# First attention: one common step of four 32-row products subtracts the maxima of the third and fourth score tile

## The chip, the cores and the metric

One core of one Trainium2 chip runs the whole program. The metric is device time in microseconds (us), the median of three runs; lower is better. All engines of the core (TensorE, VectorE, ScalarE, GpSimd, and SyncE, which issues the DMAs) run instruction streams written out in the program, tied together by semaphores.

## What is computed

Two transformer-like layers over x (4 x 512 x 128): attention over the tokens and a small context, a mixture of experts, a second attention, a second mixture. The change touches the first attention alone: 16 heads of 64, so 8 pairs of heads for each of 4 batches, 32 pairs in all.

```python
def _L0_xattn_ref(x, latents, ...):            # x: the context (4, 32, 128), latents: the tokens (4, 512, 128)
    q = lat @ Wq
    kv_input = jnp.concatenate([x, lat], axis=1)
    k, v = jnp.split(kv_input @ Wkv, 2, axis=-1)
    ...
    dots = jnp.einsum('bhid,bhjd->bhij', q, k) * scale
    attn = jax.nn.softmax(dots, axis=-1)
    out = jnp.einsum('bhij,bhjd->bhid', attn, v)
    return out @ Wout
x = x + _L0_xattn_ref(...)
x = x + _L0_ffn_ref(...)
x = x + _L1_xattn_ref(...)
x = x + _L1_ffn_ref(...)
```

## The kernel before

**Order of the work.** The loop over the pairs i = 0 to 31 is one list, order_a, from which every engine's program takes its own steps. The string ITERATION sets the order in a pair; a name stands for a step of pair i (scores s0 to s3), of the next pair (qk, top scores t0 to t4, mt for max_turn) or of the pair before (pv p0 to p3, rows in even pairs from 2 on):

```python
"E A B PC CA0 C CA1 O0 ADD CS V qk p0 p1 t0 s0 t1 p2 t2 D s1 t3 p3 t4 P0 P2 s2 s3 rows mt O1 OUT O2 O3"
```

The other names are steps that come only in some pairs: PC and CS (the context's part), V (values of the next batch), B (the router's logits), OUT (the output projection), P0 and P2 (spreading one over the sums), C and D (layer norms and turns).

**Banks.** PSUM has 8 banks of 512 columns. Each step in TAKES_BANKS gets the next of three pairs of banks in turn (0 and 1, 2 and 3, 4 and 5), one bank for each head of a pair. Before it writes, TensorE waits for whoever last reads those banks (claim and release). s2, s3, mt and the next taker follow each other in this turn, so the next taker gets the banks of s2.

**The steps of a pair.** qk (L1423 to L1425, function three) makes queries and keys as three fp32r products of split numbers each; ScalarE rounds them (QH, KH, and QF: L843, L844, L847), VectorE forms the remainders (KL, QL: L1244, L1247). top (L1598, and L1605 for the context) computes the scores once with rounded numbers, VectorE takes the maxima over them (TOPS, L1254, L1256). max_turn combines them into one number for a query and head (TOPT, L1265, VectorE) and turns them into rows with four transposes (L1612, TensorE); ScalarE evicts them as TOPROW (L852). TOPT holds the first head's maximum at one column and the second head's 64 columns on, so that in TOPROW row 0 of each half of 64 rows is that head's maximum.

scores (L1631) makes one key tile of 128 keys of exact scores, transposed: four steps of two products, one for each head, on rows 0 to 63 and rows 64 to 127 of the array. Steps 0 to 2 are KH with QH, KL with QH and KH with QL; step 3 subtracts the maximum, as the product of MINUS (-1 in row 0 of each half, else 0) with TOPROW:

```python
lhs = (KH[r, k, c], KL[r, k, c], KH[r, k, c], MINUS[r, :])[step]
rhs = (QH[r, k, :], QH[r, k, :], QL[r, k, :], TOPROW[r, i % GROUP, :])[step]
last = pe.matmul(PSUM[:, place + h, :], lhs, rhs, start=step == 0, stop=step == 3)
```

ScalarE takes the exponential of each finished tile (PT, L866) from its two banks. GpSimd adds the exponentials of a pair over the key tiles (PSUMS, L690). pv (L1663) multiplies them with the values; rows (L1693, L1699, L1707) sums them; out (L1729) projects. context_scores (L1649) and context_sums (L1680) do the same for the 32 context rows; context_scores uses MINUS too.

**Constants.** GpSimd makes MINUS_F with one selection for each half (L593), ScalarE rounds it to MINUS (L820), both in the first 20 us.

Of the kernel before, what the change touches and what calls it, by code (L numbers as in the profile page):

```python
# [6 lines left out]
F32R = mybir.dt.float32r  # L7
I32 = mybir.dt.int32
U32 = mybir.dt.uint32
ALU = mybir.AluOpType  # L10
ACT = mybir.ActivationFunctionType
AX = mybir.AxisListType

P = 128
# [27 lines left out]
def build(nc, x, ctx, lnm_g, lnm_b, lnl_g, lnl_b, Wq, Wkv, Wout, rw, rb, w1, w2, cq, ckv, cc, Wr, Wg, Wu, Wd, out):  # L42
# [3 lines left out]
    DH = 64  # L46
# [6 lines left out]
    TPB = S // P  # L53
    NT = B * TPB
    KT = S // P
# [12 lines left out]
    GROUP = 4  # L68
# [5 lines left out]
    with ExitStack() as stack:  # L74
        def sb(name, *shape, dt=F32):
            return stack.enter_context(nc.sbuf_tensor(name, [P, *shape], dt))
# [14 lines left out]
        IDENT = sb("IDENT", P)  # L91
# [11 lines left out]
        KCF = sb("KCF", PAIRS, P)  # L103

        TOPS = sb("TOPS", TPB, 2, 2)
        TOPT = sb("TOPT", P + 16 * TPB)
        MINUS = sb("MINUS", P, dt=F32R)


        with ExitStack() as queries:  # L110
            QF = queries.enter_context(nc.sbuf_tensor("QF", [P, GROUP, S], F32))
            TOPROW = queries.enter_context(nc.sbuf_tensor("TOPROW", [P, GROUP, S], F32R))
# [14 lines left out]
        MINUS_F = PT[:, 2, 1, 0:P]  # L127
# [70 lines left out]
        PSUM = stack.enter_context(nc.psum_tensor("PSUM", [P, 8, BANK], F32))  # L198
# [13 lines left out]
        def dram(name, rows, width):  # L212
# [19 lines left out]


        CONST = Steps(sem("consts"), ["ident0", "ident", "half", "ones", "empty", "numbers", "topt", "minus0", "rows0", "spread0",
                                      "minus1", "minus2", "rows1", "rows", "rows_c0", "rows_c1", "rows_c", "iota2", "iota1",
                                      "spread1", "spread", "tie", "lower", "incl0", "incl", "run", "next"])
        s_lin = sem("lin")
        s_jp = sem("jp")
# [26 lines left out]
        s_const_r = sem("rounded_consts")  # L265
# [5 lines left out]
        s_top, s_max, s_comb = sem("top_scores"), sem("half_max"), sem("row_max")  # L271
        s_topt, s_toprow = sem("max_turned"), sem("max_rows")
        s_sc, s_exp = sem("scores"), sem("exps")
# [60 lines left out]
        for b in range(B + 1):  # L334
            i = b * PAIRS
# [13 lines left out]
            for g in (2 * b - 1, 2 * b):  # L349
                if g >= 0:  # L350

                    k = GROUP * (g + 1) + 1
# [35 lines left out]
        last = 2 * B - 1  # L388
# [18 lines left out]
        order_a, place, out_at, sums_at = [], 0, {}, {}  # L407
# [164 lines left out]
        def pool_program(pool):  # L572
# [7 lines left out]
            for which in range(2):  # L580
                last = pool.iota(NUMBERS[which], [[P, LIST_ROWS[which] // P]], base=(which + 1) * N, channel_multiplier=1)
# [3 lines left out]
            def constants():  # L585
                pool.memset(TOPT[:, :], 0.0).then_inc(CONST.sem, 1)
                pool.memset(MINUS_F, 0.0).then_inc(CONST.sem, 1)
                pool.memset(ROWS_F[:, :, :], 1.0).then_inc(CONST.sem, 1)
                pool.memset(SPREAD_F, 0.0).then_inc(CONST.sem, 1)

                for k in range(2):
                    pool.wait_ge(*CONST.at(0, f"minus{k}"))
                    pool.affine_select(out=MINUS_F, in_=MINUS_F, compare_op=ALU.not_equal, fill=-1.0, base=-64 * k,  # L593
                                       pattern=[[0, P]], channel_multiplier=1).then_inc(CONST.sem, 1)

                pool.wait_ge(*CONST.at(0, "rows0"))
                pool.memset(ROWS_F[:, 0:GROUP, 0:GROUP], 0.0).then_inc(CONST.sem, 1)
                pool.wait_ge(*CONST.at(0, "rows1"))
                for p in range(GROUP):
                    last = pool.memset(ROWS_F[:, p, p:p + 1], 1.0)  # L600
                last.then_inc(CONST.sem, 1)

                pool.memset(ROWS_F[:, GROUP, 0:GROUP], 1.0).then_inc(CONST.sem, 1)
                pool.wait_ge(*CONST.at(0, "rows_c0"))
                pool.affine_select(out=ROWS_F[:, GROUP, 0:GROUP], in_=ROWS_F[:, GROUP, 0:GROUP], compare_op=ALU.is_ge, fill=0.0,
                                   base=0, pattern=[[-M, GROUP]], channel_multiplier=1).then_inc(CONST.sem, 1)
                pool.wait_ge(*CONST.at(0, "rows_c1"))
                pool.affine_select(out=ROWS_F[:, GROUP, 0:GROUP], in_=ROWS_F[:, GROUP, 0:GROUP], compare_op=ALU.is_ge, fill=0.0,
                                   base=M - 1, pattern=[[M, GROUP]], channel_multiplier=-1).then_inc(CONST.sem, 1)
                pool.iota(TOKEN_INTS, [[S, B], [1, TPB]], base=0, channel_multiplier=TPB).then_inc(CONST.sem, 1)  # L610
                pool.iota(INTS[1][:, :], [[P, E * NT]], base=0, channel_multiplier=0).then_inc(CONST.sem, 1)

                for k in range(2):
                    pool.wait_ge(*CONST.at(0, f"spread{k}"))
                    for p in range(GROUP):
                        for half in range(2):
                            part = SPREAD_F[:, p, 64 * half:64 * half + 64]
                            last = pool.affine_select(out=part, in_=part, compare_op=ALU.not_equal, fill=1.0,
                                                      base=-(64 * k + 32 * half + p), pattern=[[0, 64]], channel_multiplier=1)
                    last.then_inc(CONST.sem, 1)  # L620
                for i in range(E):
                    last = pool.memset(TIE[:, :, i:i + 1], float(E - i))
                last.then_inc(CONST.sem, 1)
                pool.wait_ge(*CONST.at(0, "ones"))
                pool.affine_select(out=LOWER[:, :], in_=ONES[:, :], compare_op=ALU.is_gt, fill=0.0, base=0, pattern=[[1, P]],
                                   channel_multiplier=-1).then_inc(CONST.sem, 1)
                pool.memset(INCL[:, :, :], 1.0).then_inc(CONST.sem, 1)
                pool.wait_ge(*CONST.at(0, "incl0"))
                pool.affine_select(out=INCL[:, :, :], in_=INCL[:, :, :], compare_op=ALU.is_ge, fill=0.0, base=0,
                                   pattern=[[1, E], [-1, E]], channel_multiplier=0).then_inc(CONST.sem, 1)  # L630
                for which in range(2):
                    for i in range(E):
                        last = pool.memset(RUN[:, which, 0, i:i + 1], float(i * N))
                last.then_inc(CONST.sem, 1)
                pool.memset(NEXT[:, E - 1:E], float(N)).then_inc(CONST.sem, 1)
# [33 lines left out]
            for name, a, place, banks in order_a:  # L669
# [8 lines left out]
                elif name == "scores" and a[1] in ((1, 2, 3) if a[0] < ALL - 1 else (1,)):  # L678

                    i, kt = a  # L680
# [11 lines left out]
                elif name == "masks":  # L692
# [13 lines left out]
                    for c in range(4):  # L706
                        pool.wait_ge(*CMASKS.at(0, f"minus{c}"))
                        pool.affine_select(out=MINUSC.rearrange("p (h k) -> p h k", h=4), in_=MINUSC.rearrange("p (h k) -> p h k", h=4),
                                           compare_op=ALU.not_equal, fill=-1.0, base=-32 * c, pattern=[[-1, 4], [0, M]],
# [32 lines left out]
        def scalar_program(act):  # L742
# [73 lines left out]
            round_context_keys(0)  # L816
            split_features(0)
            round_weights(2, ld_wv)
            act.wait_ge(*CONST.at(0, "minus2"))
            act.activation(MINUS[:, :], MINUS_F, ACT.Copy).then_inc(s_const_r, 1)  # L820
            for name, a, place, banks in order_a:
                if name == "values":
                    b, kt = a
# [29 lines left out]
                elif name == "scores":  # L853
                    i, kt = a
# [19 lines left out]
                elif name == "pv" and a[1] == KT - 1:  # L874
                    i = a[0]
# [36 lines left out]
            for name, a in order_c:  # L912
# [13 lines left out]
                elif name == "c_scores":  # L926
# [3 lines left out]
                    for k in range(2):  # L930
                        act.activation(PT[:, 2 + a % 2, 2 * k:2 * k + 2, :], PSUM[:, 2 * k:2 * k + 2, :], ACT.Exp,
                                       scale=DC ** -0.5).then_inc(CPA[a].sem, 1)
# [15 lines left out]
        def vector_program(dve):  # L948
# [284 lines left out]
            for name, a, place, banks in order_a:  # L1233
# [14 lines left out]
                elif name == "top":  # L1248
                    i, c = a
# [9 lines left out]
                elif name == "max_turn":  # L1259
# [2 lines left out]
                        dve.wait_ge(s_topt, a)  # L1262
                    else:
                        dve.wait_ge(*CONST.at(0, "topt"))
                    dve.tensor_reduce(TOPT[:, 0:P].rearrange("p (h n) -> p n h", h=2)[:, 0:16 * TPB:16, :],  # L1265
                                      TOPS[:, :, :, :].rearrange("p t a h -> p t h a"), AX.X, ALU.max).then_inc(s_comb, 1)
                elif name == "one_over":
                    g, c = a
                    cols = slice(c * P, (c + 1) * P)
# [133 lines left out]
        def tensor_program(pe):  # L1403
# [142 lines left out]
            for name, a, place, banks in order_a:  # L1546
# [5 lines left out]
                elif name == "values":  # L1552
                    b, kt = a
                    k = b % 2
# [5 lines left out]
                    for n in range(2):  # L1560
                        c = slice(n * BANK, (n + 1) * BANK)
                        last = three(PSUM[:, place + n, :], XTH[:, k, cols], XTL[:, k, cols], WH[:, 2, c], WL[:, 2, c])
# [25 lines left out]
                elif name == "top":  # L1588


                    i, c = a
# [17 lines left out]
                elif name == "max_turn":  # L1609
                    pe.wait_ge(s_comb, a + 1)  # L1610
                    for t in range(TPB):
                        last = pe.transpose(PSUM[:, place, t * P:(t + 1) * P], TOPT[:, 16 * t:16 * t + P], IDENT[:, :])  # L1612
                    last.then_inc(s_topt, 1)
                    release(mine, (s_toprow, a + 1))
                elif name == "scores":
# [3 lines left out]
                    if kt == 0:  # L1619
                        pe.wait_ge(s_qkl, 2 * i + 2)  # L1620
                        if i == 0:
                            pe.wait_ge(s_const_r, 1)
                    for step in range(4):
                        if (kt, step) == (0, 3):
                            pe.wait_ge(s_toprow, i + 1)
                        for h in range(2):
                            r = slice(DH * h, DH * h + DH)
                            c = slice(kt * P, (kt + 1) * P)
                            lhs = (KH[r, k, c], KL[r, k, c], KH[r, k, c], MINUS[r, :])[step]
                            rhs = (QH[r, k, :], QH[r, k, :], QL[r, k, :], TOPROW[r, i % GROUP, :])[step]  # L1630
                            last = pe.matmul(PSUM[:, place + h, :], lhs, rhs, start=step == 0, stop=step == 3)  # L1631
                    last.then_inc(s_sc, 1)
                    release(mine, (s_exp, SCORED[name, a]))
                elif name == "context_scores":

# [264 lines left out]
```

## Time and profile before

| | us |
|---|---|
| runs | 784.04, 781.49, 780.24 (median 781.49) |
| profiled execution, its span from first to last instruction | 788.3 |
| TensorE busy in it | 706.3 |
| VectorE, ScalarE, GpSimd busy | 475.7, 378.0, 377.4 |

The profiled execution is one more execution, beside the three runs, and its own time is known by its span alone. Durations in the rows are those of one instruction or of a group; a matmul's duration runs from its issue to its last result, so that the next one starts before it ends. The granted clock is a share of TensorE's full speed, 2.4 GHz.

### The profile page before, as it was taken

The page shows a single profiled execution, that of the slowest core. Times are in us where ns is not written, and L with a number is a line of the kernel's source. Part 1 is how long each engine was busy: PE and PEld are TensorE (multiplying, and loading weights), DVE is VectorE, ACT ScalarE, POOL GpSimd, SP SyncE. Part 2 cuts the span into 40 slices and gives each one's busy share as a digit, 9 for nine tenths or more (in the row PEclk, how much of TensorE's full clock was granted, in tenths as well). Part 3 has the DMA queues.
Part 4 walks back from the last instruction along what each step waited for, and adds up shares of the span by engine and source line. Part 5 has one row for each costly group of instructions (what it writes and reads, how often), then busy time and mean ns, then how long its engine had stood idle before and what let it go on. Part 6 is the DMA issues. An engine that isn't in the chain of part 4 may idle for free.

```text
span 788.3 us, 13872 instructions
## 1 busy us (share of the span) xinstructions
PE 706.3 (90%) x4810; PEld 430.8 (55%) x4810; DVE 475.7 (60%) x966; ACT 378.0 (48%) x580; POOL 377.4 (48%) x361
## 2 busy tenths in 40 slices
PE   4899999999999999999999999997995687568991
PEld 3654555545556555556545545566995343336661
DVE  4745484585585875667477478465443386845553
ACT  4475554564654554655445444344552643223440
POOL 7264453473464475444464553634333304674552
PEclk9999999999999999999999999998998697569996
DMA  9999999990000000000030004301212500122325
GB/s 253 197 201 197 204 190 10 4 4 1 1 1 2 1 14 1 1 1 1 1 121 2 1 1 108 114 24 32 72 32 80 155 1 28 35 75 69 88 66 177
DMA packets 109867, 50.62 MB, mean 64 GB/s; under 512 B 44804, under 2 KB 103048, under 8 KB 109800
## 3 DMA queue, kind: packets, MB, share of 16 engines
q1 hardware_dynamic: 106280, 42.46, 36.0%
q0 software_dynamic: 3520, 7.27, 2.7%
q8 instruction: 42, 0.69, 0.4%
q14 instruction: 25, 0.20, 0.1%
HBM read 20.07 MB, written 29.64 MB: 63 GB/s over the span
## 4 chain that ended last, share of the span: by engine, by line
PE 74%; DVE 11%; issue 5%; ACT 3%; POOL 3%; DMA 2%; another core or an unknown queue 1%; SPq 1%; DVEq 0%; POOLq 0%; ACTq 0%
PE PSUM L1631 14%; PE PSUM L1663 13%; PE PSUM L1598 5%; PE PSUM L1463 5%; PE PSUM L1498 4%; PE PSUM L1468 4%; PE PSUM L1729 4%; PE PSUM L1423 3%; PE PSUM L1425 2%; PE PSUM L1424 2%; PE PSUM L1612 2%; PE PSUM L1605 2%; PE PSUM L1649 2%; PE PSUM L1693 2%; DVE REC L1377 1%
## 5 line engine op out<-in xcount | busy, mean ns | idle before, releaser
L866 ACT ACTIVATE PT<-PSUM 128x1024 f32<-128x1024 f32 x128 | 128.6, 1024 | 134.1 <-PE PSUM L1631 133.7
L690 POOL TENSOR_TENSOR PSUMS<-PT 128x1024 f32<-128x1024 f32 x32 | 76.0, 2376 | 210.4 <-ACT PT L866 171.4
L690 POOL TENSOR_TENSOR PSUMS<-PSUMS,PT 128x1024 f32<-128x1024 f32 x62 | 149.6, 2413 | 16.8 <-ACT PT L866 9.9
L1254 DVE TENSOR_REDUCE TOPS<-PSUM 128x2 f32<-128x1024 f32 x128 | 152.1, 1220 | 6.9 <-PE PSUM L1598 6.5
L1663 PE MATMUL PSUM<-PT,BIG 128*64 128x512 f32 x512 | 130.6, 611 | 0.0
L1209 DVE TENSOR_TENSOR SIL<-SIL,PSUM 128x256 f32<-128x256 f32 (+1 forms) x62 | 32.2, 519 | 65.7 <-ACT SIL L783 46.8
L1244 DVE TENSOR_TENSOR KL<-PSUM,KH 128x512 fp32r<-128x512 f32 x32 | 22.1, 691 | 68.2 <-ACT KH L844 67.7
L1598 PE MATMUL PSUM<-KH,QH 64*128 64x512 f32 x256 | 57.9, 449 | 4.0 <-DVE QL L1247 3.7
L1663 PEld LDWEIGHTS PSUM<-PT,BIG 128*64 128x64 f32 x512 | 28.4, 135 | 53.4 <-issue 52.0
L1598 PEld LDWEIGHTS PSUM<-KH,QH 64*128 64x128 f32 x256 | 24.2, 183 | 59.2 <-DVE TOPS L1254 24.9
L783 ACT ACTIVATE SIL<-PSUM 128x256 f32<-128x256 f32 (+1 forms) x62 | 28.6, 462 | 56.7 <-PE PSUM L1463 31.4
L1631 PE MATMUL PSUM<-QH,KH 64*128 64x512 f32 x256 | 54.8, 423 | 1.0 <-DVE QL L1247 0.7
L662 POOL DMA_INDIRECT results_d<-YS,XG x39 | 37.4, 958 | 29.4 <-DVE YS L1216 27.3
L1631 PE MATMUL PSUM<-TOPROW,MINUS 64*128 64x512 f32 x256 | 51.1, 393 | 0.0
L1631 PE MATMUL PSUM<-QH,KL 64*128 64x512 f32 x256 | 50.9, 391 | 0.0
L1631 PE MATMUL PSUM<-QL,KH 64*128 64x512 f32 x256 | 50.8, 390 | 0.0
L1463 PE MATMUL PSUM<-XGT,WS 128*128 128x128 f32 x368 | 46.8, 282 | 0.4 <-issue 0.4
L1463 PEld LDWEIGHTS PSUM<-XGT,WS 128*128 128x128 f32 x368 | 44.5, 198 | 1.0 <-issue 0.8
L1468 PE MATMUL PSUM<-BIG,XGT 128*128 x78 | 42.7, 631 | 1.9 <-DVE XGT L1201 1.9
L662 POOL DMA_INDIRECT results_b<-YS,XG x23 | 22.0, 957 | 36.9 <-DVE YS L1216 35.7
L1293 DVE TENSOR_TENSOR OT<-OT,PSUM 128x1024 f32<-128x1024 f32 x16 | 18.9, 1217 | 34.0 <-PE PSUM L1680 34.0
L655 POOL DMA_INDIRECT lists_d<-BIG,SLOT x28 | 27.2, 971 | 12.0 <-issue 7.9
(256 smaller groups left out, 1365.5 us busy)
## 6 DMA issues: line engine op xcount, KB each, us to landing
lists_d<-EMPTY SPq DMA_DIRECT2D x3, 2730.0 KB, 35.3
lists_b<-EMPTY SPq DMA_DIRECT2D x3, 2470.0 KB, 33.4
lists_d<-EMPTY SPq DMA_DIRECT2D x1, 2665.0 KB, 34.9
XG<-lists_d SPq DMA_DIRECT2D x39, 65.0 KB
lists_b<-EMPTY SPq DMA_DIRECT2D x1, 2405.0 KB, 17.2
BIG<-in_L_ffn_w SPq DMA_DIRECT2D x1, 2048.0 KB
W2ALL<-in_L_ffn_w SPq DMA_DIRECT2D x4, 512.0 KB, 6.2
PT<-results_d SPq DMA_DIRECT2D x8, 256.0 KB, 4.4
```

The lines of the kernel that those rows point to most:

```text
L662: pool.indirect_dma_start(RES[which], bass.IndirectOffsetOnAxis(ap=XG[:, g % RING, D:D + 1].bitcast(U32), axis=0), YS[:, g % 8, :], None). ...
L690: pool.tensor_tensor(PSUMS[:, i % 2], PTT[:, i % 2, 0] if kt == 1 else PSUMS[:, i % 2], PTT[:, i % 2, kt], ALU.add).then_inc(s_ps, 1)
L866: act.activation(PTT[:, i % 2, kt], PSUM[:, place:place + 2, :], ACT.Exp, scale=DH ** -0.5).then_inc(s_exp, 1)
L1209: dve.tensor_tensor(sl, sl, up, ALU.mult).then_inc(s_hid, 1)
L1254: dve.tensor_reduce(TOPS[:, c, 0, :], PSUM[:, place:place + 2, :], AX.X, ALU.max).then_inc(s_max, 1)
L1463: last = pe.matmul(PSUM[:, bank + n, c:c + P], WS[:, 2 * (g % 2) + n, c:c + P], XGT[:, g % 3, :], start=True, stop=True)
L1468: last = pe.matmul(PSUM[:, bank, :], XGT[:, g % 3, :], WGUALL[:, bass.ds(column[1][j], BANK)], start=True, stop=True)
L1498: last = pe.matmul(PSUM[:, bank, 0:D], hidden[:, f * P:(f + 1) * P], weights[:, f * D:][:, bass.ds(column[which][j], D)], start=f == 0, st ...
L1598: last = pe.matmul(PSUM[:, place + h, :], QH[r, i % 2, c * P:(c + 1) * P], KH[r, i % 2, :], start=True, stop=True)
L1631: last = pe.matmul(PSUM[:, place + h, :], lhs, rhs, start=step == 0, stop=step == 3)
L1663: last = pe.matmul(PSUM[DH * h:DH * h + DH, 6, :], V[:, b % 2, kt, cols], PTT[:, i % 2, kt, h, :], start=kt == 0, stop=kt == KT - 1)
L1729: last = pe.matmul(PSUM[:, place, t * P:(t + 1) * P], OT[:, (GROUP * a + c) % OTS, t * P:(t + 1) * P], WOUT[:, (GROUP * a + c) % PAIRS, :] ...
```

## The change

Tiles s0 and s1 keep their four steps. For s2 and s3 only the steps 0 to 2 are made in place. Behind the third step of s3 come four products of 32 rows each: rows 0 to 31 and 64 to 95 (the two heads) add the subtraction to the banks of s2, rows 32 to 63 and 96 to 127 to the banks of s3. Only behind these is either tile told as finished. For this each maximum stands twice in TOPROW, 32 rows apart: TOPT gets it by two reductions in place of one. MINUS, for the 64-row products, has -0.5 in both rows; the new MINUS_32, for the 32-row ones, has -1. GpSimd makes four selections for it instead of two, and ScalarE one copy more. TOPT's columns are 8 apart for the four token tiles instead of 16.

```diff
-                                      "minus1", "minus2", "rows1", "rows", "rows_c0", "rows_c1", "rows_c", "iota2", "iota1",
+                                      "minus1", "minus2", "minus3", "minus4", "rows1", "rows", "rows_c0", "rows_c1", "rows_c", "iota2", "iota1",
@@ gpsimd, constants
-                for k in range(2):
+                for k in range(4):
                     pool.wait_ge(*CONST.at(0, f"minus{k}"))
-                    pool.affine_select(out=MINUS_F, in_=MINUS_F, compare_op=ALU.not_equal, fill=-1.0, base=-64 * k,
+                    pool.affine_select(out=MINUS_F, in_=MINUS_F, compare_op=ALU.not_equal, fill=-0.5, base=-32 * k,
                                        pattern=[[0, P]], channel_multiplier=1).then_inc(CONST.sem, 1)
@@ scalar
-            act.wait_ge(*CONST.at(0, "minus2"))
-            act.activation(MINUS[:, :], MINUS_F, ACT.Copy).then_inc(s_const_r, 1)
+            act.wait_ge(*CONST.at(0, "minus4"))
+            act.activation(MINUS[:, :], MINUS_F, ACT.Copy)
+            act.activation(MINUS_32[:, :], MINUS_F, ACT.Copy, scale=2.0).then_inc(s_const_r, 1)
@@ vector, max_turn
-                    dve.tensor_reduce(TOPT[:, 0:P].rearrange("p (h n) -> p n h", h=2)[:, 0:16 * TPB:16, :],
-                                      TOPS[:, :, :, :].rearrange("p t a h -> p t h a"), AX.X, ALU.max).then_inc(s_comb, 1)
+                    for k in range(2):
+                        last = dve.tensor_reduce(TOPT[:, 0:P].rearrange("p (a n) -> p n a", n=32)[:, 0:8 * TPB:8, k:4:2],
+                                                 TOPS[:, :, :, :].rearrange("p t a h -> p t h a"), AX.X, ALU.max)
+                    last.then_inc(s_comb, 1)
@@ tensor, max_turn
-                        last = pe.transpose(PSUM[:, place, t * P:(t + 1) * P], TOPT[:, 16 * t:16 * t + P], IDENT[:, :])
+                        last = pe.transpose(PSUM[:, place, t * P:(t + 1) * P], TOPT[:, 8 * t:8 * t + P], IDENT[:, :])
@@ tensor, scores
-                    for step in range(4):
+                    for step in range(4 if kt < 2 else 3):
...
-                    last.then_inc(s_sc, 1)
+                    if kt < 2:
+                        last.then_inc(s_sc, 1)
+                    elif kt == KT - 1:
+
+                        for j, at in enumerate((place_of_2, place)):
+                            for h in range(2):
+                                r = slice(DH * h + 32 * j, DH * h + 32 * j + 32)
+                                last = pe.matmul(PSUM[:, at + h, :], MINUS_32[r, :], TOPROW[r, i % GROUP, :], start=False, stop=True)
+                            last.then_inc(s_sc, 1)
+                    place_of_2 = place
                     release(mine, (s_exp, SCORED[name, a]))
```

How the instructions stand. First TensorE at the end of pair 3, before: the third tile (s2), the fourth (s3), the transposes of max_turn and the next step, here the values of the next batch (V; behind it comes qk). Of an instruction's two inputs the moving one stands first. "exps" is the semaphore of the exponentials, "half_max" that of the maxima, "row_max" that of TOPT.

```order
L1631 MATMUL PSUM<-QH,KH 128x512
L1631 MATMUL PSUM<-QH,KL 128x512 x2
L1631 MATMUL PSUM<-QL,KH 128x512 x2
L1631 MATMUL PSUM<-TOPROW,MINUS 128x512 x2
L1631 MATMUL PSUM<-QH,KH 128x512 [waits half_max]
L1631 MATMUL PSUM<-QH,KH 128x512
L1631 MATMUL PSUM<-QH,KL 128x512 x2
L1631 MATMUL PSUM<-QL,KH 128x512 x2
L1631 MATMUL PSUM<-TOPROW,MINUS 128x512 x2
L1612 MATMUL PSUM<-IDENT,TOPT 128x128 [waits row_max,half_max]
L1612 MATMUL PSUM<-IDENT,TOPT 128x128 x3
L1423 MATMUL PSUM<-WH,XTH 128x512 [waits features_dve,exps]
```

The same place of the changed program:

```order
L1635 MATMUL PSUM<-QH,KH 128x512
L1635 MATMUL PSUM<-QH,KL 128x512 x2
L1635 MATMUL PSUM<-QL,KH 128x512 x2
L1635 MATMUL PSUM<-QH,KH 128x512 [waits half_max]
L1635 MATMUL PSUM<-QH,KH 128x512
L1635 MATMUL PSUM<-QH,KL 128x512 x2
L1635 MATMUL PSUM<-QL,KH 128x512 x2
L1643 MATMUL PSUM<-TOPROW,MINUS 128x512 x4
L1616 MATMUL PSUM<-IDENT,TOPT 128x128 [waits row_max,half_max]
L1616 MATMUL PSUM<-IDENT,TOPT 128x128 x3
L1427 MATMUL PSUM<-WH,XTH 128x512 [waits features_dve,exps]
```

Two products of the third tile and two of the fourth became four together (L1643), behind all other steps of both. The step that waits for the exponentials stands where it stood, right behind the transposes.

VectorE in an early pair, before:

```order
L1254 TENSOR_REDUCE TOPS<-PSUM 128x2 [waits top_scores] x3
L1256 TENSOR_REDUCE TOPS<-PSUM 128x2x4 [waits top_scores]
L1265 TENSOR_REDUCE TOPT<-TOPS 128x4x2 [waits max_turned,half_max]
L1244 TENSOR_TENSOR KL<-PSUM,KH 128x512 [waits qk_high]
L1247 TENSOR_TENSOR QL<-PSUM,QH 128x512 [waits qk_high]
```

and in the changed program:

```order
L1256 TENSOR_REDUCE TOPS<-PSUM 128x2 [waits top_scores] x3
L1258 TENSOR_REDUCE TOPS<-PSUM 128x2x4 [waits top_scores]
L1268 TENSOR_REDUCE TOPT<-TOPS 128x4x2 [waits max_turned,half_max]
L1268 TENSOR_REDUCE TOPT<-TOPS 128x4x2
L1246 TENSOR_TENSOR KL<-PSUM,KH 128x512 [waits qk_high]
L1249 TENSOR_TENSOR QL<-PSUM,QH 128x512 [waits qk_high]
```

One reduction is added behind the first, and nothing else moved.

## Rows read from the trace of the kernel before

**Rows 1.** The page: span, busy time by engine, chain, the exponentials (mean ns of one).

```profile
span 788.3 us, 13872 instructions
...
PE 706.3 (90%) x4810; PEld 430.8 (55%) x4810; DVE 475.7 (60%) x966; ACT 378.0 (48%) x580; POOL 377.4 (48%) x361
...
PE 74%; DVE 11%; issue 5%; ACT 3%; POOL 3%; DMA 2%; another core or an unknown queue 1%; SPq 1%; DVEq 0%; POOLq 0%; ACTq 0%
...
L866 ACT ACTIVATE PT<-PSUM 128x1024 f32<-128x1024 f32 x128 | 128.6, 1024 | 134.1 <-PE PSUM L1631 133.7
```

**Rows 2.** Busy time in one stretch: PE, PEld, DVE, ACT, POOL, granted clock, DMA share, GB/s.

```profile
30.00:508.00 478.00, 473.20 (x3289) 261.51 (x3290) 305.12 (x432) 251.73 (x348) 241.41 (x124) 1.00 0.45 52
```

**Rows 3.** Timeline, end of pair 19: start, us, engine, line, operation, [idle before <-releaser].

```profile
324.69 0.40 PE L1631 MATMUL PSUM<-TOPROW,MINUS 64*128 64x512 f32 x2
...
324.71 0.17 DVE L1265 TENSOR_REDUCE TOPT<-TOPS 128x8 f32<-128x16 f32 x1
...
325.13 1.96 ACT L866 ACTIVATE PT<-PSUM 128x1024 f32<-128x1024 f32 x2 [0.97 <-PE PSUM L1631]
...
325.40 0.39 PE L1631 MATMUL PSUM<-QL,KH 64*128 64x512 f32 x2
...
325.63 0.40 PE L1631 MATMUL PSUM<-TOPROW,MINUS 64*128 64x512 f32 x2
...
325.95 0.65 PE L1612 MATMUL PSUM<-IDENT,TOPT 128*128 128x128 f32 x4
...
326.34 0.19 PEld L1423 LDWEIGHTS PSUM<-WH,XTH 128*128 128x128 f32 x1
326.37 0.47 PE L1423 MATMUL PSUM<-WH,XTH 128*128 128x512 f32 x1
```

**Rows 4.** Timeline, end of pair 20, the same columns.

```profile
338.86 1.06 PE L1693 MATMUL PSUM<-PSUMS,ROWS_F 128*32 128x512 f32 x8
...
339.74 1.03 PE L1699 MATMUL PSUM<-PTC,ROWS_F 128*32 128x512 f32 x4
```

**Rows 5.** The chain, 300 to 340 us: start, length, engine, line, instructions.

```profile
312.56 0.44 PE PSUM L1419 x4
...
318.32 0.43 PE PSUM L1598 x2
318.75 0.93 PE PSUM L1631 x8
319.68 0.23 PE PSUM L1598 x2
...
326.02 0.59 PE PSUM L1612 x4
```

**Rows 6.** Timeline, second attention, products on groups of 32 rows.

```profile
626.54 1.04 PE L1813 MATMUL PSUM<-PTC 32*128 32x512 f32 x8
```

**Rows 7.** Timeline, early: TensorE waits for an eviction of its banks.

```profile
34.31 1.03 ACT L827 ACTIVATE BIG<-PSUM 128x1024 f32<-128x1024 f32 x1 [0.81 <-PE PSUM L1425]
...
35.45 0.21 PEld L1598 LDWEIGHTS PSUM<-KH,QH 64*128 64x128 f32 x2 [0.26 <-ACT BIG L827]
35.48 0.49 PE L1598 MATMUL PSUM<-KH,QH 64*128 64x512 f32 x2
```

**Rows 8.** Timeline, end of pair 31.

```profile
507.65 1.95 ACT L866 ACTIVATE PT<-PSUM 128x1024 f32<-128x1024 f32 x2 [0.52 <-PE PSUM L1631]
...
509.96 0.12 PEld L1707 LDWEIGHTS PSUM<-PT,ROWS_F 128*32 128x32 f32 x2
```

**Rows 9.** Timeline, the first 32 us: constants, and two waits of TensorE.

```profile
11.14 0.72 POOL L593 TENSOR_SCALAR_AFFINE_SELECT PT<-PT 128x128 f32<-128x128 f32 x2
...
15.42 0.29 ACT L820 ACTIVATE MINUS<-PT 128x128 fp32r<-128x128 f32 x1
...
26.68 0.63 PE L1612 MATMUL PSUM<-IDENT,TOPT 128*128 128x128 f32 x4 [0.82 <-DVE TOPT L1265]
...
31.24 0.50 PE L1631 MATMUL PSUM<-QH,KH 64*128 64x512 f32 x2 [0.73 <-DVE QL L1247]
```

More of the change, by code:

```diff
@@ L105, in build @@
         TOPS = sb("TOPS", TPB, 2, 2)
-        TOPT = sb("TOPT", P + 16 * TPB)
+        TOPT = sb("TOPT", P + 8 * TPB)
         MINUS = sb("MINUS", P, dt=F32R)
+        MINUS_32 = sb("MINUS_32", P, dt=F32R)
         with ExitStack() as queries:
```

## The prediction, made before the changed kernel had run

> **What bounds the kernel now.** I read the page first: its busy times and the chain that ended last. TensorE is busy 706.3 of 788.3 us, the next engine 475.7, and 74% of the chain is TensorE [rows 1]. Then the first attention by itself: in the 478 us from 30 to 508, TensorE is busy 473.20, so it idles 4.8 us in all, at a granted clock of 1.00, which is the 2.4 GHz level [rows 2]. So in this stage time is TensorE's time: whatever is taken off its queue is gained, and whatever makes it wait is lost, with at most 4.8 us of idle time to soak it up.
>
> Third, the timeline where one head pair ends, for this is where the change acts. In an odd pair [rows 3] the last step of the third score tile starts at 324.69 and ends at 325.09, and ScalarE starts that tile's exponential at 325.13. The fourth tile's last two steps start at 325.40 and 325.63, 0.23 us apart, and end at 326.03. Behind them come only the four transposes of max_turn (325.95) and at once the next taker of banks, here the values of the next batch, whose first weight load is at 326.34 and whose first product ends at 326.37 + 0.47 = 326.84. It writes the banks of the third tile, since the three bank pairs go round (third tile, fourth tile, max_turn, next taker), and so waits for the third tile's exponential. That one ended at 325.13 + 1.02 = 326.15, with the 1024 ns of one from the page [rows 1]. TensorE is thus let go 0.19 us before it needs it. After an even pair there is cover instead: the sum rows take 1.06 us (every fourth pair another 1.03) ahead of the transposes [rows 4], and at some pairs the output projection comes behind them.
>
> **The change part by part.**
>
> *One step less.* Three steps remain for the fourth tile and three for the third; one common step of four products serves both. Two products of 64 rows run side by side and the next two follow 0.23 us later, so a step costs 0.23 us: the eight products of a tile take 0.93 in the chain [rows 5]. Four products on four groups of 32 rows also run together: in the second attention eight instructions of 32x512, four fp32 products of two instructions each, take 1.04 us [rows 6]. That is 0.13 us an instruction, where one of this width in turn takes no less than the 0.23 of an fp32r step, so they must overlap. I take one step for the four here. That removes 0.23 us for each of 32 pairs.
>
> *A change of shape.* The common step has 32-row products behind 64-row ones. No row shows 64x128 followed by 32x128. The rows nearest to it are other changes of shape: the first two 64x128 products behind 128x64 ones take 0.43 us in the chain, the same two behind 64x128 ones 0.23; four 128x128 transposes take 0.59 behind 64-row products and 0.44 behind 128x128 ones [rows 5]. So 0.15 to 0.20 us for a change, 0 if 64 to 32 rows is none. I take 0.20, because the common step has 512 columns, as the row of 0.43 has. The change back to 128 rows was there already (64 to 128) and is paid once before and once after. So the common step ends 0.43 us behind the step ahead of it, and the whole block ends 2 x 0.23 - 0.43 = 0.03 us earlier than before, not 0.23. The Trainium skill (TensorEngine Tiling (Array Packing), Key Properties) says that changing the tiling mode drains the engine, which goes against this change; the trace agrees, with 0.43 against 0.23. By the page's rule the sum would be the one that I take, without it that of the first rival.
>
> *The third tile's exponential comes late.* Before, the third tile was whole one tile ahead of the fourth; now both are whole together. In the times of rows 3: the last of the six steps ends at 325.79 - 0.23 = 325.56 (325.79 being 325.40 + 0.39), the common step at 325.99. The exponential starts 0.04 later, at 326.03, and ends at 327.05. From the end of an eviction to the weight load that waited for it are 0.11 us (35.34 to 35.45), and from that load to the end of the first product 0.52 (to 35.97) [rows 7]. So the next taker's load is at 327.16 and its first product ends at 327.68, against 326.84: **0.84 us later for each pair without cover**. The saved step is in this already. What is queued behind the waiting step on TensorE is all of the next pair; ScalarE and VectorE wait for it in turn, so nothing is caught up. The fourth tile's exponential now ends near 327.98 and the row maxima's eviction near 328.6, while the six products of a step like this one (or of qk) end at 327.68 + 5 x 0.23 = 328.83; ScalarE is free just in time, and I add nothing.
>
> *Where there is no cover.* Sum rows come in even pairs from 2 on. So the 15 odd pairs 1 to 29 are without, and pair 0: 16 places. There the next taker is qk, in some the values or the router's logits; all of them get the third tile's banks and wait the same. 16 x 0.84 = 13.4 us. In the 15 even pairs 2 to 30 the sum rows put 1.0 us more between the block and the next taker, 0.31 + 1.0 = 1.3 us [rows 4], and the exponential needs 327.16 - 326.03 = 1.13 from the old end; they keep the 0.03: -0.5 us.
>
> *Pair 31.* The last pair's products that sum over the third and fourth exponentials loaded at 509.96, with the exponentials over at 507.65 + 1.95 = 509.60 [rows 8]. These end 0.88 later now (0.90 from the late start, about 0.02 less), at 510.48, and the load comes 0.11 later, at 510.6 instead of 509.96. Part of these 0.6 us lay behind other products, so I take half: +0.3 us once.
>
> *VectorE.* The maxima are written by two reductions instead of one, 0.17 us more for each pair [rows 9]. In the steady pairs they are done before the transposes' turn: that of rows 3 has its transposes at 325.95 and the reduction over by 324.88, one more makes 325.05. Only for pair 0 did TensorE wait for them [rows 9]: +0.17 us once. *Constants.* Two more selections on GpSimd (0.36 us each) and one more copy on ScalarE (0.29) lie in the first 20 us [rows 9]. The matrix is ready at 11.86, with two more at 12.6, ScalarE takes it up at 15.42, and its first use is in the tile that starts at 31.24. If that cover were gone they would cost 1.0 us; I count nothing. No DMA and no queue entry of SP moves.
>
> **Sum.** 13.4 - 0.5 + 0.3 + 0.2 = **+13.4 us**. On the profiled execution's span, 788.3, that gives 801.7. The runs shown are 780.24 to 784.04 us with a median of 781.49: this profiled execution was 0.9% above the median, so I add the sum, which lies in a stage at full clock, to the median: 794.9 us, 1.7% slower. A measurement here tells about 0.5% (3.9 us) from no change.
>
> **Rivals.**
> 1. *Slower, but no drain.* If 64 to 32 rows costs nothing, the common step ends 0.20 us earlier everywhere: 16 x 0.64 - 15 x 0.23 + 0.3 = +7.1, 788.6 us. For it: the columns stay at 128, and in no row does the number of rows alone go from 64 to 32. Against it: every change of shape in rows 5 costs 0.15 or more.
> 2. *Faster: the exponential's delay is covered.* Bank claims would not be what TensorE meets first; then only the saved step is left, -0.23 x 32 = -7.4, 774.1 us, if the shape change is free as well. It decides at one place, the step behind the transposes: the cover from the old end of the fourth tile is 326.34 - 326.03 = 0.31 us in odd pairs, and the exponential needs 1.13. Only if that gap were 0.8 us wider would it be so; the order of the program shows the wait for the exponentials on just this product.
> 3. *No change.* Covered, but with the drain: -0.03 x 32 = -1 us, 780.5. The change then doesn't do what it says, since the step it saves is paid back in the drain.
> 4. *Much slower: the four products don't run together.* With fp32r they might go two and two: +0.23 x 32 = 7.4 more, 802.3; one by one 3 x 7.4 = 22 more, 817. Rows 6 speak against it, though for fp32.
> 5. *The clock.* Each new gap is some 0.6 us in 13; if the granted clock fell for it, more than 10 us would be added. Against: it is 1.00 over the whole stage although that has a gap of 0.73 us [rows 9, 2].
>
> **How the numbers follow.** Forecast 0.72, rival 1 0.12, rival 2 0.04, rival 3 0.04, rival 4 0.06, rival 5 0.02. The range takes in rival 1 and, above, 0.3 us more per uncovered pair (a slower release or a larger drain, 16 x 0.3 = 5): 787 to 800, with the runs' own scatter of some 2 us below. Faster 0.04 (rival 2), within 0.5% 0.06 (rival 3 and half as much again for delays taken up in the 4.8 us of idle), slower 0.90.
>
> **What would show it.** The two exponentials of the third and fourth tile start 0.9 us later relative to the steps; the four products of the common step lie at one start time, and end 0.43 behind the step before (0.23 in rival 1, twice that or more in rival 4). Sixteen times TensorE idles 0.5 to 0.7 us behind the transposes, released by the exponential, so its idle time in this stage grows from 4.8 by about 10 us, while its busy time falls. If those gaps are not there, the forecast is wrong at its largest term; if they are there and the time is not longer, something behind them gave it back.

## The result

| | before | changed |
|---|---|---|
| median of the runs, us | 782.21 | 797.73 |
| lowest and highest | 780.24, 784.04 | 796.01, 801.21 |
| ratio, 95% interval | | 1.0204 (1.0176 to 1.0232) |
| span of the profiled execution | 788.3 | 794.2 |

The changed kernel is 15.5 us slower (13.8 to 18.1 by the interval), 2.0%. The forecast was 794.9 us, 13.4 us slower. The two spans differ by 5.9 us only, because the profiled execution of the kernel before spent 279.8 us on what comes after the stage of the change and that of the changed kernel 269.9, at mean granted clocks of 0.85 and 0.87. The traces are therefore compared up to the end of that stage, and the runs for the whole.

The page of the changed kernel, the lines that answer to [rows 1]:

```profile
span 794.2 us, 13909 instructions
...
PE 705.1 (89%) x4810; PEld 424.4 (53%) x4810; DVE 475.1 (60%) x998; ACT 376.7 (47%) x581; POOL 377.7 (48%) x363
```

Over the whole execution TensorE is busy for as long as before. The first attention, same columns as [rows 2]:

```profile
30.00:508.00 478.00, 463.16 (x3164) 247.90 (x3162) 300.66 (x443) 244.42 (x341) 234.16 (x122) 1.00 0.53 49
```

In the same 478 us TensorE idles 14.8 us now instead of 4.8, and gets 3164 of its instructions done instead of 3289. The granted clock is 1.00 as before, the 2.4 GHz level. From 30 us to the end of the stage (508.54 us before, 524.34 now) the idle time is 4.8 and 14.8 us too, and the busy time 473.7 and 479.5. The waits name what it idles for, in 13 places for this line (engine, line, releaser; total us, times, longest):

```profile
PEld PSUM L1427 <- ACT PT L868: 10.6, 13, 0.8
```

In the other three places, behind pairs 13, 21 and 29, the next taker of banks is the router's logits (L1757). In each of the sixteen TensorE's products stand still for 0.56 to 0.62 us behind the transposes; behind the even pairs 2 to 30 they don't stand still there at all.

The end of pair 19, to be held against [rows 3]; it lies 10.3 us later because of the pairs before it:

```profile
335.04 0.25 DVE L1268 TENSOR_REDUCE TOPT<-TOPS 128x8 f32<-128x16 f32 x2
...
335.49 0.40 PE L1635 MATMUL PSUM<-QL,KH 64*128 64x512 f32 x2
335.82 0.19 PEld L1643 LDWEIGHTS PSUM<-TOPROW,MINUS 32*128 32x128 f32 x4 [0.36 <-issue]
335.82 0.50 PE L1643 MATMUL PSUM<-TOPROW,MINUS 32*128 32x512 f32 x4
...
336.25 0.66 PE L1616 MATMUL PSUM<-IDENT,TOPT 128*128 128x128 f32 x4
336.36 1.94 ACT L868 ACTIVATE PT<-PSUM 128x1024 f32<-128x1024 f32 x2 [1.86 <-PE PSUM L1643]
337.45 0.19 PEld L1427 LDWEIGHTS PSUM<-WH,XTH 128*128 128x128 f32 x1 [0.78 <-ACT PT L868]
...
337.48 0.47 PE L1427 MATMUL PSUM<-WH,XTH 128*128 128x512 f32 x1 [0.57 <-ACT PT L868]
```

All four products of the common step run at once: they start at 335.82 and end at 336.32, 0.43 us behind the end of the step ahead of them (335.89). ScalarE starts the third tile's exponential at 336.36, 0.04 behind the block, and the fourth tile's right behind it (the row holds both, 1.94 us). The transposes end at 336.91, and then TensorE has nothing to do until 337.48, when the third tile's exponential lets it go. From the end of the block (336.32) to the first weight load of the next taker are 1.13 us; before they were 0.31.

To see where the time goes I took the end of the last product of each pair's fourth tile in both traces, and its shift from one kernel to the other. The table sorts the shift by what lies in between; in pairs 6, 10, 14, ..., 30, seven of them and called spread pairs here, VectorE multiplies the spread sums in (P0, P2) just ahead of the last tiles. The rows of the last pair in the changed kernel:

```profile
523.84 0.51 PE L1643 MATMUL PSUM<-TOPROW,MINUS 32*128 32x512 f32 x4
524.38 1.03 ACT L868 ACTIVATE PT<-PSUM 128x1024 f32<-128x1024 f32 x1 [1.41 <-PE PSUM L1643]
```

They end at 524.34, and in the kernel before they ended at 508.54, so the shift is 15.8 us. (508.54 is 0.04 ahead of the fourth exponential of that pair; before, too, ScalarE starts 0.04 behind the products.) How the shift grows:

| where | what is added to the shift, us | sum |
|---|---|---|
| up to pair 0 | 1.39 | 1.39 |
| from pair 0 to 1, and from each odd pair to the next even one, 16 times | 0.80 to 0.90, and 1.03 to 1.13 into pairs 6, 10, ..., 30 | 15.03 |
| from each even pair to the next odd one, 15 times | -0.22 to +0.12, most -0.02 to -0.06 | -0.62 |

The -0.22 stands from pair 6 to 7. Every other trace below has 0.2 us less there than at its neighbours too, the one without any part of the change among them (cover_old), so it belongs to the one trace of the kernel before that all are compared with.

Of the 1.39 us at the start, 0.08 belongs to the maxima (below). Most of the rest is the pace of TensorE in the first 23 us: in this execution it turned from slow to fast products 3.4 us later than in the other, which shows in the four products at the 20th us:

```profile
20.05 1.22 PE L1602 MATMUL PSUM<-KH,QH 64*128 64x512 f32 x4
```

against 0.73 us in the kernel before:

```profile
20.15 0.73 PE L1598 MATMUL PSUM<-KH,QH 64*128 64x512 f32 x4
```

The view prints a granted clock of 1.00 for all of it, but the trace's own record of the clock begins only at 19.53 us in the kernel before and at 22.97 in the changed one, in each where the products turn fast. Ahead of that both have products of 128x512 that take 0.63 us and follow 0.43 us apart, behind it 0.39 to 0.40 us, 0.23 apart. The same two paces stand in the run uncovered, below, at recorded clocks of 0.50 and 1.00. So the slow stretch ran at the lower level, 1.2 GHz, and it lasted 3.4 us longer here. Four of the other kernels below have the 0.73 us, and cover_old, in which nothing of the change is left, has 1.22 us: this belongs to the execution and not to the change.

### The profile page after: what moved, and what is told of

It reads as the page before. It is cut to its first block and busy times, and to the rows that moved or that the text cites. A ratio compares the mean times of both kernels' runs of the same rounds, so it can differ in the third digit from the quotient of the medians.

```text
span 794.2 us, 13909 instructions
## 1 busy us (share of the span) xinstructions
PE 705.1 (89%) x4810; PEld 424.4 (53%) x4810; DVE 475.1 (60%) x998; ACT 376.7 (47%) x581; POOL 377.7 (48%) x363
## 5 line engine op out<-in xcount | busy, mean ns | idle before, releaser
L1676 PE MATMUL PSUM<-PT,BIG 128*64 128x512 f32 x512 | 130.6, 611 | 0.0
L1676 PEld LDWEIGHTS PSUM<-PT,BIG 128*64 128x64 f32 x512 | 28.4, 135 | 53.5 <-issue 52.1
L1427 PE MATMUL PSUM<-XTH,WH 128*128 128x512 f32 x64 | 27.6, 431 | 7.8 <-ACT PT L868 5.5
```

The source lines that it names most:

```text
L1676: last = pe.matmul(PSUM[DH * h:DH * h + DH, 6, :], V[:, b % 2, kt, cols], PTT[:, i % 2, kt, h, :], start=kt == 0, stop=kt == KT - 1)
```

## The experiments

The theory: the loss is TensorE's wait for the late exponential of the third tile, at the 16 places where no other work lies between, and the common step saves nothing because it costs a change of shape. Rivals: the common step itself is dear, in every pair alike (15.5 / 32 = 0.48 us); the doubled reduction delays the transposes; the wait would turn up at another step if it were covered at this one. All experiments are edits of the changed kernel, cover_old of the kernel before. Their diffs are cut to what matters (`...`). "Stage" below is the shift of pair 31's last product against the kernel before, from the traces, as in the table above.

### The common step in the covered pairs alone (covered)

```diff
-                    for step in range(4 if kt < 2 else 3):
+                    joint = i % 2 == 0 and i > 0
+                    for step in range(3 if joint and kt >= 2 else 4):
...
-                    if kt < 2:
+                    if kt < 2 or not joint:
```

> The common step only in the 15 even pairs 2 to 30, which have sum rows behind it; the other pairs keep the old four steps. Theory (the loss is the wait for the late exponential where nothing covers it): the seven pairs that spread one over the sums just ahead lose about 0.2 us each, because there the fourth tile's start is set by VectorE and the shape change is paid without a saved step, the other eight gain 0.03: +1 us against the kernel before. Rival (the common step itself is dear, 15.5 us / 32 = 0.48 in every pair): +7 us.

Measured: 783.8 against 780.81 us, ratio 1.0056 (1.0032 to 1.0080), so 2.5 to 6.2 us. Stage: +1.15. The stage behaves as expected: the shift grows by 0.18 to 0.22 us at each of the seven spread pairs and by -0.04 to 0.00 at the other even ones from pair 4 on. The rows of spread pair 18 show why the saved step is no gain there:

```profile
306.27 0.39 PE L1636 MATMUL PSUM<-QL,KH 64*128 64x512 f32 x2
...
306.67 0.21 PEld L1636 LDWEIGHTS PSUM<-QH,KH 64*128 64x128 f32 x2 [0.45 <-DVE OT L1290]
...
306.70 0.50 PE L1636 MATMUL PSUM<-QH,KH 64*128 64x512 f32 x2
...
307.60 0.51 PE L1644 MATMUL PSUM<-TOPROW,MINUS 32*128 32x512 f32 x4
```

The fourth tile's banks are those of the spread's first product, and VectorE is still multiplying out of them. The third tile is a step shorter, TensorE comes 0.23 us earlier and only waits longer; then it pays for the change of shape. The runs put the loss higher than the stage, at least 1.3 us above it, so that the theory's 1 us lies outside their interval as well. Where the rest is, the traces don't show (the span is 781.5 us here and 781.1 in no_common, below). The mean granted clock of these eight runs is 0.952, of the 13 of the kernel before 0.955, which may be it and isn't shown to be. Against the rival's 7 us the run decides all the same: it lies outside the interval.

### The common step in the uncovered pairs alone (uncovered)

The same edit as in covered, with another condition:

```diff
+                    joint = i % 2 == 1 or i == 0
```

> The common step only in pair 0 and the odd pairs, where the next taker of banks comes right behind the transposes. Theory: 16 x 0.84 + 0.3 = +13.7 us against the kernel before, nearly all of the change's loss. Rival (0.48 in every pair alike): 17 x 0.48 = +8 us.

Measured: 796.55 us, ratio 1.0208 (1.0182 to 1.0233), 14.2 to 18.2 us. Stage: +14.6, of which 1.6 us came in one single pair, 22. There the granted clock fell to its lower level for 3.41 us (busy time of PE, PEld, DVE, ACT, POOL, granted clock, DMA share, GB/s):

```profile
360.00:366.90 6.90, 6.33 (x51) 4.04 (x50) 5.45 (x9) 3.83 (x5) 3.48 (x2) 1.00 0.00 0
366.92:370.33 3.41, 3.41 (x9) 2.63 (x10) 2.58 (x4) 1.45 (x3) 3.27 (x2) 0.50 0.01 2
```

and the products of 128x512 there took 0.63 us, 0.43 apart, instead of 0.40, 0.23 apart; one from inside and one from just behind it:

```profile
367.21 0.63 PE L1428 MATMUL PSUM<-WL,XTH 128*128 128x512 f32 x1
...
370.73 0.40 PE L1428 MATMUL PSUM<-XTL,WH 128*128 128x512 f32 x1
```

Just before, TensorE had waited 0.57 us for the exponential and then made eight small products of 8 columns. The changed kernel has the same wait in the same place and its clock stayed at 1.00, and in no other of these traces did it fall inside the stage. Without these 1.6 us the stage is +13.0. The runs' interval again lies above the theory's 13.7, by 0.5 us at least. Half the common steps make nearly the whole loss. The rival's 8 us is excluded.

### The same lateness without saving and without change of shape (late64)

```diff
-                                r = slice(DH * h + 32 * j, DH * h + 32 * j + 32)
-                                last = pe.matmul(PSUM[:, at + h, :], MINUS_32[r, :], TOPROW[r, i % GROUP, :], start=False, stop=True)
+                                r = slice(DH * h, DH * h + DH)
+                                last = pe.matmul(PSUM[:, at + h, :], MINUS[r, :], TOPROW[r, i % GROUP, :], start=False, stop=True)
```

> The subtraction of both tiles again with four products of 64 rows in two steps, but both behind the other steps of both tiles: nothing saved, no change of shape, only the third tile finished late, 0.23 us ahead of the fourth instead of 0.93. Theory: the next taker's load comes at the old end + 0.94 instead of + 0.31, so 16 x 0.63 = +10 us. Rival (only the 32-row shape costs): 0.

Measured: 794.83 us, ratio 1.0184 (1.0156 to 1.0211), 12.2 to 16.5 us. Stage: +11.0. The end of pair 19:

```profile
331.95 0.63 PE L1643 MATMUL PSUM<-TOPROW,MINUS 64*128 64x512 f32 x4
...
332.39 1.94 ACT L868 ACTIVATE PT<-PSUM 128x1024 f32<-128x1024 f32 x2 [1.67 <-PE PSUM L1643]
...
333.48 0.19 PEld L1427 LDWEIGHTS PSUM<-WH,XTH 128*128 128x128 f32 x1 [0.56 <-ACT PT L868]
```

The four products end at 332.58, the load comes 0.90 later, not 0.31. The steps of the shift out of uncovered pairs are 0.59 to 0.68, as expected, and 0.84 to 0.93 into the seven spread pairs, which I had again left out. So the order of the work alone, with as many products of the same shapes as before, makes more than two thirds of the loss. The theory's 10 us lie below the runs' interval, as in the two runs above, and what the runs have above the stage stays open here too.

### The change of shape alone (shape)

`joint` is False throughout, so every tile keeps its four steps:

```diff
-                    for step in range(4 if kt < 2 else 3):
+                    joint = False
+                    for step in range(3 if joint and kt >= 2 else 4):
...
+                            if (kt, step) == (KT - 1, 3):
+                                r = slice(DH * h, DH * h + 32)
-                            lhs = (KH[r, k, c], KL[r, k, c], KH[r, k, c], MINUS[r, :])[step]
+                            lhs = (KH[r, k, c], KL[r, k, c], KH[r, k, c], (MINUS_32 if (kt, step) == (KT - 1, 3) else MINUS)[r, :])[step]
```

> Everything in its old place, but the fourth step of the fourth tile is two products of 32 rows instead of two of 64. Theory: 64 to 32 rows is a change of shape like the others, 0.2 us in each of 32 pairs: +6.4 us. Rival (no drain between 64 and 32 rows, the four products together are what takes long): 0.

Measured: 788.51 us, ratio 1.0107 (1.0078 to 1.0136), 6.1 to 10.6 us. Stage: +7.9, of which 2.2 were there at pair 0, where this execution turned fast late as well (1.22 us for the four products at the 20th us). From pair 0 to 31 the shift grows by 5.7 us, in 28 of the 31 pairs by 0.16 to 0.25.

```profile
331.13 0.39 PE L1638 MATMUL PSUM<-QL,KH 64*128 64x512 f32 x2
331.45 0.18 PEld L1638 LDWEIGHTS PSUM<-TOPROW,MINUS 32*128 32x128 f32 x2 [0.36 <-issue]
331.45 0.50 PE L1638 MATMUL PSUM<-TOPROW,MINUS 32*128 32x512 f32 x2
```

Two 32-row products end 0.43 us behind the 64-row step (331.52 to 331.95), just as four do in the changed kernel. The price is thus that of the change of shape and not of the number of products; a step of the same shape costs 0.23.

### Everything but the common step (no_common)

```diff
-                    for step in range(4 if kt < 2 else 3):
+                    joint = False
+                    for step in range(3 if joint and kt >= 2 else 4):
...
-                    if kt < 2:
+                    if kt < 2 or not joint:
```

> The changed kernel's constants, its maxima at two places and its two reductions on VectorE, but all steps in their old places and shapes, no common step. Theory: these are hidden but for 0.2 us in pair 0: 0 to +0.5 us against the kernel before. Rival (the second reduction delays the transposes in every pair): 32 x 0.17 = +5 us.

Measured: 781.99 us against 782.03, ratio 0.9998 (0.9982 to 1.0014). Stage: +0.03, made of 0.21 at pair 0 and the -0.19 at pair 7 that every trace has. The 0.21 is not the price of the maxima: covered and uncovered have the same constants and reductions and stand at -0.02 and +0.07 at pair 0. What the second reduction does cost shows in TensorE's one wait for it, in pair 0, which is 0.90 us in all kernels with two reductions and 0.82 in both with one ([rows 9]). The row of the changed kernel:

```profile
27.93 0.63 PE L1616 MATMUL PSUM<-IDENT,TOPT 128*128 128x128 f32 x4 [0.90 <-DVE TOPT L1268]
```

Constants, doubled maxima and reductions are free but for this 0.08 us.

### Other work put over the wait (cover_common, cover_old)

In the odd pairs 1 to 29 p3 goes behind the fourth tile:

```diff
+        moved = list(ITERATION)
+        moved.remove("p3")
+        moved.insert(moved.index("mt"), "p3")
         for i in range(ALL):
-            for at in ITERATION:
+            for at in moved if i % 2 and i < ALL - 1 else ITERATION:
```

> The changed kernel, but in the odd pairs 1 to 29 the last part of pv (p3, four products, about 1.0 us) stands behind the fourth tile instead of between t3 and t4, so that the next taker of banks comes 1.0 us later. Theory: the exponential is over by then, and against cover_old (the same move in the kernel before) only pair 0 (0.84), the seven spread pairs (0.2 each) and pair 31 remain: about +2 us, in place of 15.5. Rival (something else than the late exponential holds TensorE, or it is waited for at a later step too): the difference stays above 10 us.

> The kernel before with the same move of p3 in the odd pairs 1 to 29: the control of cover_common. Without p3 between them, the top products t3 and t4 and the third tile follow each other closely and may wait for VectorE's maxima and for the exponential of the second tile: 0 to +0.4 us a pair, 0 to +6 us against the kernel before. Only the difference between the two kernels bears on the theories.

Measured: cover_common 795.14 us, ratio to the kernel before 1.0154 (1.0126 to 1.0181); cover_old 790.74, ratio 1.0093 (1.0067 to 1.0118). Between the two 4.4 us by the medians, and 3.9 us in the stage (+13.3 and +9.4). With six runs of each, scattered over 5 and 8 us, the 4.4 is known to some 3 us. The end of pair 19 in cover_common:

```profile
334.53 0.51 PE L1646 MATMUL PSUM<-TOPROW,MINUS 32*128 32x512 f32 x4
...
334.97 1.08 PE L1679 MATMUL PSUM<-PT,BIG 128*64 128x512 f32 x4
335.07 1.94 ACT L871 ACTIVATE PT<-PSUM 128x1024 f32<-128x1024 f32 x2 [2.58 <-PE PSUM L1646]
335.98 0.42 PEld L1619 LDWEIGHTS PSUM<-IDENT,TOPT 128*128 128x128 f32 x4 [0.81 <-issue]
335.98 0.66 PE L1619 MATMUL PSUM<-IDENT,TOPT 128*128 128x128 f32 x4
...
336.37 0.19 PEld L1430 LDWEIGHTS PSUM<-WH,XTH 128*128 128x128 f32 x1
```

The exponentials start as late as in the changed kernel, but the next taker's load follows the transposes without a wait. Against its control the common step now adds -0.07 to +0.25 us a pair, the spread pairs' 0.20 to 0.25 among them, but for four. From pair 0 to 1, where nothing was moved, it adds 0.82. From pair 29 to 30 it adds 0.91. 0.2 of this is the spread; the other 0.7 is a second wait, for VectorE's remainder of the queries, in cover_old and in cover_common:

```profile
494.16 0.21 PEld L1601 LDWEIGHTS PSUM<-KH,QH 64*128 64x128 f32 x2 [0.38 <-DVE QL L1250]
...
497.90 0.21 PEld L1605 LDWEIGHTS PSUM<-KH,QH 64*128 64x128 f32 x2 [1.08 <-DVE QL L1252]
```

It comes from the late exponentials as well. Behind them on ScalarE stands the copy of one over the sums (RECS), which starts 2.12 us behind the fourth tile in cover_old (489.23) and 2.81 in cover_common (492.95); VectorE waits for that copy and does the remainders after it. In pairs 3, 11 and 19 (0.33, 0.20 and 0.19) the load of the fourth tile waits 0.45 us for VectorE's maxima where the control's waits 0.20 to 0.22: a saved step in front of a wait, as in the spread pairs. Pair 3 has some 0.1 of the context's scores besides. In pair 28 (0.34) the third tile's load waits 0.26 us for an exponential, and the control's doesn't.

The difference fell from 15.5 to 4.4 us, so most of the loss goes away with the cover, though not all that I expected (2 us). Of the rival's second wait one pair in fifteen has some, and the difference is well under its 10 us. The move itself is a bad one: cover_old loses 7.3 us (5.2 to 9.2 by the interval of the ratio; the medians are 8.7 apart) to the kernel before, so this is a test and no repair. No version beat the kernel before, and none can by much as long as the change of shape costs 0.20 of the 0.23 us that the common step saves.

## Why the prediction was right, and where its sum was off

*The uncovered pairs*, 0.84 us each. This was the sum's main term, and it measured 0.80 to 0.90 in the nine places that lead to no spread pair. The other seven measured 1.03 to 1.13, with the spread's 0.2 in them. The times that rows 3 and 7 gave were right to a few hundredths: from the block's new end to the load 327.16 - 325.99 = 1.17 us forecast, 1.12 to 1.18 measured in the sixteen places. That the term stands for the late exponential is shown by uncovered, late64 and cover_common. Of the signs named for it the gaps came, and the idle time grew by 10.0 us, as forecast; the busy time was to fall and rose by 5.8 us. The busy time of PE doesn't show what was saved, since it has no gap at a change of shape (in pair 19 the common step starts at 335.82 and the step ahead of it ends at 335.89).

*The change of shape*, 0.20. Forecast from other shapes, measured as 0.20 from 64 to 32 rows (shape). Rival 1, without a drain, falls: it would have had the block end 0.20 us sooner in every pair. The Trainium skill's statement that a change of tiling mode drains the engine (TensorEngine Tiling (Array Packing), Key Properties) holds for a change in the rows alone too, in these runs at 0.43 against 0.23 us.

*Four products in one step*. Right; rival 4 falls, with a common step of 0.50 us for four as for two.

*The even pairs keep the 0.03 us.* This was the step that failed in part: seven of the fifteen lose 0.20. In the spread pairs the fourth tile waits for VectorE, and a saved step in front of a wait is not saved. It could have been read in the trace of the kernel before, where the load of that tile in pair 18 has its wait already:

```profile
306.18 0.22 PEld L1631 LDWEIGHTS PSUM<-QH,KH 64*128 64x128 f32 x2 [0.21 <-DVE OT L1286]
```

and in the changed kernel the same load reads:

```profile
316.29 0.21 PEld L1635 LDWEIGHTS PSUM<-QH,KH 64*128 64x128 f32 x2 [0.45 <-DVE OT L1290]
```

0.21 became 0.45, the whole step. Seven times 0.23 are 1.6 us that the sum lacked. Without them its 13.4 lies just below the interval of the runs (13.8 to 18.1), with them it is 15.0, and the runs show 15.5. The stage's 15.8 is no better match than this: 1.3 of it is the slow start of one execution, and from pair 0 on it is 14.4.

*Pair 2* has the context's scores behind its transposes, which now wait for the fourth tile's exponential:

```profile
70.49 0.21 PEld L1662 LDWEIGHTS PSUM<-QF,KCF 64*32 64x32 f32 x16 [0.26 <-ACT PT L868]
```

Its 0.12 us was not in the sum; covered has it too (0.15), uncovered, with the old steps in pair 2, has not (-0.03).

*Maxima and constants.* Forecast 0.17 us at pair 0, by the time of one reduction; the wait there grew by 0.08, since two in a row take 0.25 and one 0.17. *Pair 31*, 0.3. The load of its sums comes 2.03 us behind the fourth tile instead of 1.42, the 0.6 that was forecast. The next products of exponentials with values (L1663 before, L1676 now) start 3.87 us behind it instead of 3.66, so 0.2 of it stays.

*The clock*, rival 5. In the changed kernel's trace the new gaps did not lower it: 1.00 over the stage. In uncovered, which has the same gaps, it fell once and cost 1.6 us. The rival's price, more than 10 us, came nowhere, but the mechanism is not nothing, and of the runs without a trace only their mean clock over the whole is known. Rivals 2 and 3, with the delay covered, fall with the same rows. With the cover built in (cover_common against cover_old) most of the loss is gone, as they would have had it, though a rest of 4.4 us stays.

## What to carry to other kernels

Count what is saved between waits, not on the engine: a product that completes a buffer can't be put off without putting off its reader, and if the buffer's next writer stands close behind on the same engine, the engine waits for that reader. Here a step of 0.23 us was saved and each such pair took 0.84 us longer. Before steps of different tile shapes are merged, set the price of the change of shape (0.20 us here) against the step (0.23 us). And look at each kind of iteration by itself: the pairs differed in what stood behind the block and in front of it, and a saving in front of a wait for another engine is none. Behind one late step look along the other engines too: in one pair the late exponentials came back to TensorE through ScalarE's and VectorE's queues, 0.7 us.

## What the runs showed of the hardware

Going from products on 64 rows to products on 32 rows, the columns unchanged, costs 0.20 us, as much as a change from 128x64 to 64x128. Two and four fp32r products on groups of 32 rows take the same 0.50 us. And the moment at which TensorE's clock first reaches its upper level differs from one execution to the next, from 18.16 to 24.18 us in these nine traces: it moved pair 0 by over 1 us. Until then the view prints 1.00, and only the products show the lower level, 0.63 us for 128x512 instead of 0.39 to 0.40.
